# Layer 0's attention in another order: shift before normalise, turned probabilities before the denominators, output product last

## What is computed

```python
x = x + tanh(g_xattn[0]) * L0_xattn(layernorm(x), ctx, ctx, ...)   # 16 heads of width 8
x = x + tanh(g_ffn[0])   * L0_ffn(layernorm(x), ...)               # 8 experts, the 2 largest of each row
x = x + tanh(g_xattn[1]) * L1_xattn(layernorm(x), ctx, ctx, ...)   # one head, causal
x = x + tanh(g_ffn[1])   * L1_ffn(layernorm(x), ...)               # experts choose their rows
# L0_xattn:
scores  = einsum('bhqd,bhkd->bhqk', qh, kh) / sqrt(8)
attn    = softmax(scores)
context = einsum('bhqk,bhkd->bhqd', attn, vh)
return context.reshape(...) @ w_out + b_out
```

## Time and profile before

| | |
|---|---|
| median of 3 runs | 1081.37 us (1080.57 to 1089.81) |
| the profiled execution | 1083.73 us, span 1081.9 us |
| busy over the span | PE 88%, DVE 56%, ACT 54%, POOL 64% |
| mean granted PE clock | 0.955 |
| layer 0's attention loop | from about 20 us to about 327 us |
| the stages behind it | about 755 us |

### The profile page before, as it was taken

One profiled execution on the slowest core, in us unless ns is written; L12 is line 12 of the kernel. 1 busy time (PEld: TensorE's weight loads), 2 busy tenths in 40 slices (PEclk: granted clock), 3 DMA queues, 4 the chain that ended last, 5 costly groups with the idle time before them and its releaser, 6 DMA issues.

```text
span 1081.9 us, 25309 instructions
## 1 busy us (share of the span) xinstructions
PE 951.4 (88%) x8941; PEld 796.5 (74%) x8941; DVE 605.3 (56%) x1554; ACT 583.0 (54%) x1258; POOL 687.2 (64%) x909
## 2 busy tenths in 40 slices
PE   4999998798767999899989989887799999999990
PEld 2777776576657998899979978775577876877880
DVE  4898889988953562144514548885635424433320
ACT  2887786577524444444544657654445455444440
POOL 5655465578737777177507777731586756778885
PEclk9999998899868999999999999999999999999995
DMA  8354332011144677677667774213164643655553
GB/s 350 97 161 147 115 113 88 26 44 48 52 149 152 207 215 244 194 214 208 211 195 209 238 241 155 68 51 104 10 115 45 93 69 43 104 61 52 62 54 44
DMA packets 132829, 136.58 MB, mean 126 GB/s; under 512 B 33634, under 2 KB 103650, under 8 KB 131810
## 3 DMA queue, kind: packets, MB, share of 16 engines
q1 hardware_dynamic: 102482, 97.52, 28.3%
q0 software_dynamic: 28928, 29.91, 17.4%
q10 hardware_dynamic: 1296, 7.54, 1.7%
HBM read 49.81 MB, written 49.62 MB: 92 GB/s over the span
## 4 chain that ended last, share of the span: by engine, by line
PE 50%; DVE 11%; DMA 10%; ACT 9%; issue 8%; POOL 7%; SPq 4%; POOLq 0%; ACTq 0%; DVEq 0%
PE psum L777 9%; PE psum L787 8%; PE psum L948 7%; PE psum L958 7%; DMA work<-w_sb 3%; ACT w_sb L1556 3%; PE psum L620 3%; DMA odd<-ln_sb,dest 3%; PE psum L912 2%; DMA out_x<-ln_sb,dest 2%; POOL xg L1834 2%; SPq L461 2%; DMA work<-xg 2%; DVE w_sb L1075 1%; ACT lnT L1528 1%
## 5 line engine op out<-in xcount | busy, mean ns | idle before, releaser
L1636 ACT ACTIVATE hid_sb<-psum,work 128x128 f32<-128x128 f32 (+1 forms) x424 | 145.5, 411 | 161.6 <-PE psum L777 161.5
L1849 POOL DMA_INDIRECT work<-yg,place x128 | 128.7, 1006 | 89.6 <-issue 61.2
L777 PE MATMUL psum<-work 128*128 128x128 f32 (+1 forms) x848 | 153.7, 325 | 9.9 <-DMA work<-w_sb 7.7
L787 PE MATMUL psum<-w_sb,hid_sb 128*128 x1192 | 151.0, 276 | 0.0
L787 PEld LDWEIGHTS psum<-w_sb,hid_sb 128*128 128x128 f32 x1192 | 145.3, 193 | 2.1
L777 PEld LDWEIGHTS psum<-work 128*128 128x128 f32 x848 | 125.1, 194 | 23.6 <-DMA work<-w_sb 13.0
L1925 POOL DMA_INDIRECT out_x<-ln_sb,dest x68 | 106.3, 1563 | 47.8 <-DVE ln_sb L1476 29.9
L948 PE MATMUL psum<-work,w_sb 128*128 128x272 f32 (+2 forms) x512 | 131.4, 398 | 4.7 <-ACT work L1716 2.4
L1262 DVE TENSOR_TENSOR yg_sb<-psum,work 128x128 f32<-128x128 f32 (+1 forms) x106 | 36.6, 346 | 170.1 <-PE psum L787 170.1
L1925 POOL DMA_INDIRECT odd<-ln_sb,dest x68 | 105.6, 1554 | 39.9 <-DVE ln_sb L1476 21.3
L1750 ACT ACTIVATE ctx_sb<-psum,w_sb 128x272 f32<-128x272 f32 (+2 forms) x256 | 115.4, 487 | 24.8 <-PE psum L948 19.9
(11 more groups left out here) (214 smaller groups left out, 1773.9 us busy)
## 6 DMA issues: line engine op xcount, KB each, us to landing
work<-w_sb SPq DMA_DIRECT2D x106, 322.0 KB
work<-xg SPq DMA_DIRECT2D x73, 128.0 KB
yg<-yg_sb SPq DMA_DIRECT2D x73, 128.0 KB
xg<-yg_sb SPq DMA_DIRECT2D x24, 384.0 KB, 4.0
ctx_sb<-tok SPq DMA_DIRECT2D x8, 1088.0 KB, 6.1
ctxn<-sums_sb SPq DMA_DIRECT2D x64, 64.0 KB
out_x<-x_sb SPq DMA_DIRECT2D x16, 256.0 KB
odd<-yg_sb SPq DMA_DIRECT2D x10, 384.0 KB, 2.7
```

What stands on the lines that cost most here:

```text
L777: e.matmul(banks[UP_BANKS[c]][:, 0:cols], w1g(b)[:, c * P:c * P + P], xgT_sb[:, u % 2, at:at + cols], start=True, stop=True).then_inc(s_up, 1)
L787: ins = e.matmul(banks[DOWN_BANKS[b % 2]][:, n * D:n * D + D], hid0[:, b % 2, c, n * P:n * P + P], w2_sb[:, bass.ds(number, 1), c, :].rear ...
L1636: e.activation(hid0[:, b % 2, c, 0:cols], banks[UP_BANKS[c]][:, 0:cols], ACT.Gelu, bias=w1g(b)[:, HID + c:HID + c + 1]).then_inc(s_hg, 1)
L1849: e.indirect_dma_start(dst[:, k, :], None, yg_dram[h], at, bounds_check=NROWS[h] - 1, oob_is_err=False).then_inc(s_get[i], 16)
```

## The change

No operation is added or removed. In iteration p

- PE: turn_p of chunks 0 and 1 goes ahead of spread_rden and logits, and output goes from the middle to the end, behind the transposes of turn or turn_router0;
- DVE: shift goes ahead of normalise, stats_router ahead of add_output (and so to the pair p - 4 in place of p - 3), and the second place for routing steps ahead of add_output;
- ACT: copy_p of chunks 0 and 1 goes ahead of copy_logits;
- POOL: moments for s_momr goes from iterations 7, 11, ..., 31 to 8, 12, ..., 32.

```diff
--- before.py
+++ after.py
@@ -726,20 +726,18 @@
                     attend(p - 2)
                 if p < NP:
                     values(p)
-                if 0 <= p - 3 < NP:
-                    spread_rden(p - 3)
+                if 0 <= p - 1 < NP:
+                    turn_p(p - 1, (0, 1))
                 if p % 2 == 0 and 0 <= (p - 6) // 2:
                     w.wait_ge(s_wrc, 1)
                     logits((p - 6) // 2, ROUTER, B_P, wrc[:, 0:NE], s_lnTr, s_lgm, s_lg)
-                if 0 <= p - 1 < NP:
-                    turn_p(p - 1, (0, 1))
+                if 0 <= p - 3 < NP:
+                    spread_rden(p - 3)
                 if g < NG:
                     if p % 2 == 0:
                         project_k(g)
                     else:
                         project_q(g)
-                if 0 <= p - 3 < NP:
-                    output(p - 3)
                 if 0 <= p - 1 < NP:
                     turn_p(p - 1, (2, 3))
                 for h in range(NPARTS - 1):
@@ -751,6 +749,8 @@
                     center_router()
                 if p % 2 == 1 and 0 <= (p - 5) // 2:
                     turn_router0((p - 5) // 2)
+                if 0 <= p - 3 < NP:
+                    output(p - 3)
                 if p == NP:
                     turn_weights()
                 if p == NP + 1:
@@ -1214,18 +1214,20 @@
                     largest(p)
                 for _ in range(steps[0]):
                     next(side, None)
-                if 0 <= p - 3 < NP:
-                    normalise(p - 3)
                 if p < NP:
                     shift(p)
                 if 0 <= p - 3 < NP:
-                    add_output(p - 3)
+                    normalise(p - 3)
+                stats0(20 + 2 * p, 2)
+                if 0 <= p - 4:
+                    stats_router(p - 4)
                 for _ in range(steps[1]):
                     next(side, None)
-                stats0(20 + 2 * p, 2)
+                if 0 <= p - 3 < NP:
+                    add_output(p - 3)
                 if 0 <= p - 2 < NP:
                     invert(p - 2)
-                if 0 <= p - 3 < NP:
+                if p == NP + 2:
                     stats_router(p - 3)
                 for _ in range(steps[2]):
                     next(side, None)
@@ -1601,10 +1603,10 @@
                     copy_sums(p - 2)
                 if p < NP:
                     values(p)
+                if 0 <= p - 1 < NP:
+                    copy_p(p - 1, (0, 1))
                 if p % 2 == 0 and 0 <= (p - 6) // 2:
                     copy_logits((p - 6) // 2)
-                if 0 <= p - 1 < NP:
-                    copy_p(p - 1, (0, 1))
                 if g < NG:
                     if p % 2 == 0:
                         keys(g)
@@ -1869,8 +1871,8 @@
                     add_bias(p)
                 if p % 4 == 3 and 2 * (p + 5) < NT:
                     moments(2 * (p + 5), TS, s_st0, 2 * (p + 5) + TS, s_mom)
-                if p >= 7 and p % 4 == 3:
-                    moments(2 * (p - 7), TS, s_st1, 2 * (p - 7) + TS, s_momr)
+                if p >= 8 and p % 4 == 0:
+                    moments(2 * (p - 8), TS, s_st1, 2 * (p - 8) + TS, s_momr)
                 for t in range(rows_by(p - 2), rows_by(p - 1)):
                     put(t)
             moments(NT - TS, TS, s_st1, NT, s_momr)
```

## The result

| | before | changed |
|---|---|---|
| time, us: median (lowest to highest) of 22 runs each | 1080.74 (1076.75 to 1089.81) | 1086.47 (1083.48 to 1089.51) |
| ratio, 95% interval | | 1.0046 (1.0033 to 1.0060) |
| profiled execution: time, span, us | 1083.73, 1081.9 | 1084.89, 1083.1 |

The change costs 5.0 us (0.0046 x 1080.74; the medians differ by 5.7). The forecast was 5 us of gain and a range that ended at 1085: wrong in direction. The two profiled executions differ by only 1.2 us, because the one of before is a late one (3.0 over its median) and the one of after an early one (1.6 under).

A forecast was written before the change was run, and what follows sets the result against it. It took PE as the bound up to iteration 17, then mostly DVE to 22, POOL from 24 to 28, DVE from 29; 0.2 us left at L(31) plus the tail's 4.9 gave 5.1 gained, median 1076.3, range 1067 to 1085.

The forecast's parts named there:

- Up to 17: PE-bound iterations: turn_p fills PE's 0.46 us hole before spread_rden; net gain 0.23 us in odd iterations, 0.08 in even.
- S(16) 2.5 sooner: Start of scores in iteration 16: 2.5 us earlier, from 0.9 in iterations 3 to 5 and 1.6 in 6 to 15.
- Iterations 18 to 23: Gain of 1.8 us at 18, loss of 0.4 at 20; L(24), the start of largest in iteration 24, 3.7 sooner.
- keys(24) 4.8 us sooner: POOL's keys of iteration 24, at 229.10 before, where POOL's stretch without idle time begins, come 4.8 us sooner.
- The 1.78 us wait before add_output in iteration 18: DVE's wait for the output product goes, with routing steps and statistics now ahead of add_output: 1.8 us gained.
- the wait of add_output in iteration 20: On DVE, add_output waits for an output now behind PE's count and turned tiles: an estimated 0.4 us lost.
- Elsewhere DVE has no idle time worth naming to give: DVE in iterations 18 to 23, apart from 18 and 20: no further gain.
- The moments: POOL's stretch from keys(24) to the end of iteration 28 holds two moments calls, not one: 4.6 of 4.8 us lost.
- The tail: From L(31), start of largest in iteration 31, to the last put_rows(33): exp starts about 6.0 after L(31); 4.9 us gained.
- Behind the loop: The 755 us behind layer 0's loop keep their order and should only shift with it.
- The first: Rival: gain carried through POOL, the 4.6 us not lost; 9.7 gained, or 11.4 if the clock's drop goes, 1070; chance 0.2.
- The last one: Rival: from 18 to 31 PE stands before output, then runs at half clock; 5.8 us slower, 1087; chance 0.1.

The follow-up runs named there:

- l_change: Changed kernel cut to layer 0's attention loop, two plain POOL operations in place of each indirect store: 344.71 us, 344.78 a second time.
- l_before: Kernel before, cut to layer 0's attention loop, two plain POOL operations in place of each indirect store: 336.71 us.
- f_moments_alone: Whole kernel before with only POOL's router moments an iteration later: 1087.56 us, ratio 1.0042 to the kernel before.
- f_new_to_16_old_from_17: Whole kernel with the change's order in iterations 0 to 16, the old order from 17, moments as before: 1080.03 us, ratio 0.9990 to before.
- the cut kernels: Kernels ended behind layer 0's loop, two plain POOL operations in place of each indirect store: before 336.71 us, changed 344.71.
- the first and the third set: First: whole kernels with parts of the change, ratios 0.9992 to 1.0020; third: changed kernel cut to layer 0's loop, one edit each, 342.82 to 346.44 us.
- the control: Changed kernel unchanged, run a second time where the kernel before took 1299.9 and 1300.4 us: ratio 0.9999.

## Why the prediction was wrong

**Up to 17: the mechanism right, its sum wrong.** The prediction had S(16) 2.5 sooner. The steady odd iterations gave 0.12 where 0.23 was forecast, the even ones nothing where 0.08 was, and iterations 3 to 5 gave 0.1 in place of 0.9 (L(3) to L(6) 21.78, before 21.87). Counted from L(0), so that the start of each run doesn't matter, L(14) is 0.6 sooner in l_change than in l_before (104.5 against 105.1), iterations 15 and 16 together then take 0.84 more (16.67 against 15.83; last section), and at L(17) nothing is left (129.5 against 129.3). That the profile shows L(17) 1.7 sooner than before is the clock's fall in iteration 14, 1.67 us, which the changed kernel's trace doesn't have.

**The step that failed: "Iterations 18 to 23", and with it keys(24) 4.8 us sooner.** It went wrong twice.

First, its largest term was a gain against a disturbance. The 1.78 us wait before add_output in iteration 18 was counted as the old order's. PE there, in the kernel before, ran at half clock:

```profile
163.81 1.38 PE L620 MATMUL psum<-ident,w_sb 128*128 128x128 f32 x8
164.99 1.91 PE L582 MATMUL psum<-ctx_sb,w_sb 128*128 128x512 f32 x2
166.70 1.06 PE L653 MATMUL psum<-w_sb,ctxn 128*128 128x128 f32 x4
```

In l_before, at full clock in that place, the same wait is:

```profile
164.69 0.48 DVE L1098 SCALAR_TENSOR_TENSOR x_sb<-psum,tg_sb,x_sb 128x256 f32<-128x256 f32 x1 [0.22 <-PE psum L658]
```

and L(18) to L(19) is 9.43, not 11.59. The prediction took the fall in iteration 14 as an event that may come or not, and read the one in 18 as structure. It is a common event: of the seven traces with the old order from 17 on, four have an iteration 18 of 11.2 to 11.8 and three one of 9.4. The changed kernel's trace has the fall too (project_k 2.08) and a wait of 1.22 there, so in this pair the term came to 1.2 of 1.8; without a fall on either side it is 0.2 (9.24 in l_change against 9.43 in l_before). The rows around showed the half clock; the row alone did not.

Second, it priced the wait of add_output in iteration 20 at 0.4, "an estimate". It is 2.14 us in the changed trace (2.06 in l_change), and there is another of 1.99 in iteration 23, of which the half clock behind PE's gap made about 1.4. "Elsewhere DVE has no idle time worth naming to give" was right, and missed the other side: an engine without idle time can only lose. The prediction worked out when the product fits behind the shift in an iteration that PE bounds, and not what "last on PE" means when DVE is the bound: from one product through the scores and PE's whole next iteration to the next product is a loop of its own, and where PE's iteration holds the count and its wait for ACT it takes longer (from 175.37 to 186.80, 11.4 us, in l_change, an estimated 1.4 of it by the half clock, from 1.22 and 2.01 in place of 0.71 and 1.12) than what DVE has to do. L(24) came 1.2 later where 3.7 sooner was forecast, keys(24) 0.4 later where 4.8 sooner was: 4.9 and 5.2 us, nearly the whole error of the sum (5.1 forecast, -1.2 measured).

**The moments: right.** Forecast 4.6, measured 4.5 alone (1.0042, good to about 2 us). keys(24) to L(30) took 52.6 in f_moments_alone and 53.1 in the changed kernel (forecast 52.4, before 47.8), there with the waits for stores in iteration 25 (4.8) and 29 (2.2; forecast about 4).

**The tail: the mechanism right, its size read against a long one.** 3.5 of 4.9 in this pair, but L(31) to the last put_rows is 32.5 in f_new_to_16_old_from_17 and in f_moments_alone, both with the old order there, not 33.9: against them the gain is 2.1. exp of iteration 31 starts 6.1 behind L(31), as forecast, but behind it DVE still waits 2.33 and 1.30 for PE.

**Behind the loop: right**, within 0.7 us in all five traces.

The sum as the profiles have it: -0.36 (keys(24)) - 5.33 (to L(30)) + 0.64 (to L(31)) + 3.51 (tail) + 0.34 (behind) = -1.2. The medians differ by 5.7: the other 4.5 are the place of the two profiled executions among their runs, 3.0 over the one median and 1.6 under the other. The falls in iterations 14 and 18 (1.7 and some 2.2 us) can account for the lateness of before, though other executions have such falls too.

**The rivals.** The first needed keys(24) sooner or stores that bind less, and neither came (0.4 later, and 53.1 for POOL's stretch). The last one named the right time, 1087, and the right place, PE standing before the product. But it had the tail's gain falling to nothing and the clock at 0.6 in some ten iterations; the tail kept 2.1 to 3.5, and in the cut kernels' traces the half clock made 1.2 to 2.2 us of the stretch from 17 to 24 and the chain itself 2.6. That its sum met the measured time is in part luck.

What stays open: L(26) to the next stage is 1.5 to 2.6 shorter in the changed kernel than in f_new_to_16_old_from_17 and before, read from one trace each; of the difference between 8.0 us in the cut kernels and 5.0 in the whole one, only the two waits that replace each other are shown, not what each is worth; and the shares of chain and clock in the order's loss rest on traces of one execution each, with medians too coarse to tell them apart.

## What to carry to other kernels

Moving an operation to the end of one engine's iteration is free only where that engine is the bound; where another one is, follow the loop once round (product, next scores, whole iteration, product) and compare it with the bound's period, for each kind of iteration. Before a wait is counted as something to gain, look at the granted clock of the engine that it waits for, or at a second place or trace of the same kind: a gain against a disturbance is none. The same holds for a loss: iteration 20's came in every trace, iteration 23's in some. When a consumer and its producer's statistics are moved together, price the pair: moved alone, each half made another wait.

## What the runs showed of the hardware

In the first and the third set the kernel before took 1297 to 1300 us in place of 1081 to 1083, and the changed one 1301 in place of 1086, with a mean granted clock of 0.88 to 0.89 in place of 0.95 to 0.96. In the trace of the control PE stands 123 us in all between two instructions for no wait that the profile shows, in the trace of before 1.8 us. Nine of these gaps are of 3.5 to 18.5 us, and each lies where POOL issues indirect DMAs one per 1.3 us; in the trace of before none is over 0.5, though POOL issues them there at the same rate (1.00 us each and 0.30 between). What makes up the rest of the 220 us is not taken apart. The kernels without indirect DMAs show no such jump: 342.8 to 346.4 there, 344.7 and 344.8 for l_change elsewhere. What does this, the chip or something around it, is not shown: the chips are numbered 0, 10 and 12 where the kernel before took 1297 to 1300, and 0, 1 and 15 in the later sets where it took 1081 to 1083. It hid a difference of 5 us entirely.

PE's order can meet a gap that no wait explains. In the changed kernel it stands, in iteration 15, between the second and the third of the four transposes of one chunk, between which the program has no wait:

```profile
135.49 0.44 PE L620 MATMUL psum<-ident,w_sb 128*128 128x128 f32 x2
136.67 0.87 PE L620 MATMUL psum<-ident,w_sb 128*128 128x128 f32 x6 [0.74 <-issue]
```

The control, at 1301 us, has the same gap of 0.74 at the same instruction (136.73), and L(15) to L(16) is 8.31 or 8.32 us in every trace whose first 17 iterations have the new order, 7.47 to 7.72 in those with the old. It took back all that the iterations before had gained.
